# A decoder's self attentions: the fourth query tile finished in its own slot, the rotated keys taken one slot later

## The reference

```python
q = split_heads(x @ Wq)
k = split_heads(x @ Wk)
v = split_heads(x @ Wv)
q = _apply_rope(q, cos, sin)
k = _apply_rope(k, cos, sin)
scores = jnp.einsum('bhqd,bhkd->bhqk', q, k) * scale
scores = jnp.where(causal[None, None], NEG_INF, scores)
attn = jax.nn.softmax(scores, axis=-1)
ctx = jnp.einsum('bhqk,bhkd->bhqd', attn, v)
return ctx.reshape(b, s, H * HD) @ Wo
...
x = _layernorm(x + _L0_attn_ref(x, L0_attn_Wq, L0_attn_Wk, L0_attn_Wv, L0_attn_Wo), axis=-1)
```

## Time and profile before

| | |
|---|---|
| median of 3 runs | 2695.97 us (2695.12 to 2696.59) |
| profiled execution | 2701.27 us |
| its span | 2699.4 us |
| PE busy | 2454.4 us, 91% |
| DVE busy | 1853.7 us, 69% |
| ACT busy | 1586.2 us, 59% |
| POOL busy | 721.8 us, 27% |
| mean granted clock of PE | 0.964 |

### The profile page before, as it was taken

One profiled execution on the slowest core, in us unless ns is written; L12 is line 12 of the kernel. 1 busy time (PEld: TensorE's weight loads), 2 busy tenths in 40 slices (PEclk: granted clock), 3 DMA queues, 4 the chain that ended last, 5 costly groups with the idle time before them and its releaser, 6 DMA issues. The chain is left out here.

```text
span 2699.4 us, 58652 instructions
## 1 busy us (share of the span) xinstructions
PE 2454.4 (91%) x21584; PEld 1576.5 (58%) x21584; DVE 1853.7 (69%) x3371; ACT 1586.2 (59%) x2718; POOL 721.8 (27%) x671
## 2 busy tenths in 40 slices
PE   6888888989999999999778999999899999999974
PEld 4555555446666666666345666665466666665432
DVE  4676766657777777775556666666478888885597
ACT  4666666248778877785133555554167777774233
POOL 4565657611100111012233221214310000012201
PEclk8999998999999999999888999999999999999987
DMA  3333334516665566666340344335167777776400
GB/s 89 84 72 72 84 84 88 140 22 117 116 116 110 108 115 116 118 108 128 119 164 1 89 91 92 89 81 138 40 119 147 141 146 144 148 150 130 106 0 32
DMA packets 777604, 273.63 MB, mean 101 GB/s; under 512 B 746097, under 2 KB 748913, under 8 KB 775793
## 3 DMA queue, kind: packets, MB, share of 16 engines
q1 hardware_dynamic: 775696, 265.85, 46.8%
q0 software_dynamic: 1760, 5.77, 0.8%
HBM read 84.55 MB, written 6.44 MB: 34 GB/s over the span
## 5 line engine op out<-in xcount | busy, mean ns | idle before, releaser
L833 ACT ACTIVATE ph<-p,ri 128x1024 bf16<-128x1024 f32 (+4 forms) x512 | 437.4, 854 | 477.0 <-DVE ri L1139 398.1
L1149 DVE SCALAR_TENSOR_TENSOR pl<-p,ri,ph 128x1024 bf16<-128x1024 f32 (+4 forms) x512 | 511.9, 1000 | 141.4 <-issue 72.4
L1206 PE MATMUL ps<-wo_hi,v_hi 128*128 128x128 bf16 x2688 | 478.6, 220 | 59.7 <-DMA wo_lo<-pl 58.6
L1208 PE MATMUL ps<-wo_hi,v_lo 128*128 128x128 bf16 x2688 | 478.2, 220 | 0.0
L1207 PE MATMUL ps<-wo_lo,v_hi 128*128 128x128 bf16 x2688 | 478.1, 220 | 0.0
L844 ACT ACTIVATE p<-p,nb 128x1024 f32<-128x1024 f32 (+4 forms) x512 | 435.4, 850 | 46.3 <-DVE nb L1132 36.0
L1206 PEld LDWEIGHTS ps<-wo_hi,v_hi 128*128 128x128 bf16 x2688 | 263.5, 98 | 129.9 <-DMA wo_lo<-pl 80.7
L1206 PE MATMUL ps<-k_hi,q_hi 128*128 128x512 bf16 (+3 forms) x768 | 272.2, 354 | 36.9 <-DVE k_lo L1102 28.8
L1207 PEld LDWEIGHTS ps<-wo_lo,v_hi 128*128 128x128 bf16 x2688 | 263.7, 98 | 38.9
L1208 PE MATMUL ps<-k_hi,q_lo 128*128 128x512 bf16 (+3 forms) x768 | 271.9, 354 | 0.0
L1207 PE MATMUL ps<-k_lo,q_hi 128*128 128x512 bf16 (+3 forms) x768 | 271.9, 354 | 0.0
(11 more groups left out here) (191 smaller groups left out, 5831.8 us busy)
## 6 DMA issues: line engine op xcount, KB each, us to landing
raw_kv<-in_wkvself SPq DMA_DIRECT2D x32, 512.0 KB
raw_q<-in_wqself SPq DMA_DIRECT2D x32, 256.0 KB
wo_hi<-ph SPq DMA_TRANSPOSE x512
wo_lo<-pl SPq DMA_TRANSPOSE x512
raw_q<-in_woself SPq DMA_DIRECT2D x32, 256.0 KB
raw_q<-in_wqcross SPq DMA_DIRECT2D x32, 256.0 KB
raw_q<-in_wocross SPq DMA_DIRECT2D x32, 256.0 KB
raw_kv<-in_wkvcross SPq DMA_DIRECT2D x24, 256.0 KB
```

The costliest lines, as they stand in the source:

```text
L833: nc.scalar.activation(m["ph"][:, qt % 2, 0:w], m["p"][:, qt % 2, 0:w], ACT.Copy, scale=ri[:, qt % 2:qt % 2 + 1]).then_inc(p_norm, 1)
L1149: nc.vector.scalar_tensor_tensor(out=m["pl"][:, qt % 2, 0:w], in0=m["p"][:, qt % 2, 0:w], scalar=ri[:, qt % 2:qt % 2 + 1], in1=m["ph"][:, ...
L1206: nc.tensor.matmul(o, l(0), r(0), start=first, stop=False)
L1208: return nc.tensor.matmul(o, l(1), r(0), start=False, stop=last)
```

## The change

In the causal stages the fourth tile's `rounded` (ACT), `inverse` and `remainder` (DVE) move from slot 0 of the next unit to the end of slot 3 of their own, ahead of v and the head's output. In self0 the rotated key's `rotated` on ACT (k_hi) and on DVE (k_lo) moves from slot 2 to slot 3, behind `rounded` of tile 2 and behind `scores` of tile 3. The semaphore `tr_in[qt]` becomes two, `tr_hi[qt]` and `tr_lo[qt]`: `rounded` waits for the transposes of `ph` alone, `remainder` for those of `pl`, PE for both. `units` now runs 4 units ahead of the loop, 6 passes, and 4 units after it, in all stages with a loop.

```diff
-        tr_in = [sem(f"tr_in{i}") for i in range(QT)]
+        tr_hi, tr_lo = [sem(f"tr_hi{i}") for i in range(QT)], [sem(f"tr_lo{i}") for i in range(QT)]
...
-            unit(0, None)
-            with engine.Fori(0, 7) as it:
+            for n in range(4):
+                unit(n, None)
+            with engine.Fori(0, 6) as it:
                 for i in range(4):
-                    unit(1 + i, it)
-            for n in range(UNITS - 3, UNITS):
+                    unit(4 + i, it)
+            for n in range(UNITS - 4, UNITS):
                 unit(n, None)
...
(ACT, rounded)
-                        act.wait_ge(tr_in[bq], at(lambda n: 32 * (c["u"] + behind(n, qt, 2)[0] + 1), n, it))
+                        act.wait_ge(tr_hi[bq], at(lambda n: 16 * (c["u"] + behind(n, qt, 2)[0] + 1), n, it))
...
(ACT, unit)
-                        if n or qt:
+                        if qt or n and not L.causal:
                             rounded(*((n, it, qt - 1) if qt else (n - 1, it, QT - 1)))
+                        if L.rope and qt == QT - 1:
+                            rotated(n, it, 1, L.jobs(n, 1))
                         act.wait_ge(s_max, at(lambda n: CREDIT + c["s"] + QT * n + qt + 1, n, it))
...
+                        if L.causal and qt == QT - 1:
+                            rounded(n, it, qt)
                         job_parts(n, it, qt, L.jobs(n, qt))
                         if qt == QT - 1 and n:
                             heads_out(n - 1, it)
-                        if L.rope and qt > 0:
-                            rotated(n, it, qt - 1, L.jobs(n, qt - 1))
+                        if L.rope and qt == 1:
+                            rotated(n, it, 0, L.jobs(n, 0))
...
(DVE, unit)
-                        if n or qt:
+                        pending = qt or n and not L.causal
+                        if pending:
                             inverse(*prior)
                         scores(n, it, qt)
+                        if L.rope and qt == QT - 1:
+                            rotated(n, it, 1, L.jobs(n, 1))
                         job_parts(n, it, qt, L.jobs(n, qt), ("QN",))
-                        if n or qt:
+                        if pending:
                             remainder(*prior)
+                        if L.causal and qt == QT - 1:
+                            inverse(n, it, qt)
+                            remainder(n, it, qt)
                         job_parts(n, it, qt, L.jobs(n, qt), ("K", "KN", "Q", "V"))
                         if qt == QT - 1 and n:
                             heads_out(n - 1, it)
-                        if L.rope and qt > 0:
-                            rotated(n, it, qt - 1, L.jobs(n, qt - 1))
+                        if L.rope and qt == 1:
+                            rotated(n, it, 0, L.jobs(n, 0))
...
(PE, weigh)
-                    pe.wait_ge(tr_in[qt], at(lambda n: 32 * (c["u"] + n + 1), n, it))
+                    pe.wait_ge(tr_hi[qt], at(lambda n: 16 * (c["u"] + n + 1), n, it))
+                    pe.wait_ge(tr_lo[qt], at(lambda n: 16 * (c["u"] + n + 1), n, it))
```

More of the change, by code:

```diff
@@ L431, in transposed @@
                     sp.nop(nofuse=True)
-                    sp.dma_start_transpose(m["pT"][0][:, qt, 0:w // P, :], m["ph"][:, qt % 2, 0:w]).then_inc(tr_in[qt], 16)
+                    sp.dma_start_transpose(m["pT"][0][:, qt, 0:w // P, :], m["ph"][:, qt % 2, 0:w]).then_inc(tr_hi[qt], 16)
                     sp.wait_ge(p_lo, at(count, n, it))
                     sp.nop(nofuse=True)
-                    sp.dma_start_transpose(m["pT"][1][:, qt, 0:w // P, :], m["pl"][:, qt % 2, 0:w]).then_inc(tr_in[qt], 16)
+                    sp.dma_start_transpose(m["pT"][1][:, qt, 0:w // P, :], m["pl"][:, qt % 2, 0:w]).then_inc(tr_lo[qt], 16)
                 def unit(n, it):
@@ L863, in _ @@
                 units(act, unit, L)
-                rounded(UNITS - 1, None, QT - 1)
+                if not L.causal:
+                    rounded(UNITS - 1, None, QT - 1)
                 if L.name in EARLY:
@@ L1145, in remainder @@
                     if bn >= 0:
-                        dve.wait_ge(tr_in[bq], at(lambda n: 32 * (c["u"] + behind(n, qt, 2)[0] + 1), n, it))
+                        dve.wait_ge(tr_lo[bq], at(lambda n: 16 * (c["u"] + behind(n, qt, 2)[0] + 1), n, it))
                     dve.wait_ge(p_norm, at(lambda n: c["s"] + QT * n + qt + 1, n, it))
@@ L1180, in _ @@
                 units(dve, unit, L)
-                inverse(UNITS - 1, None, QT - 1)
-                remainder(UNITS - 1, None, QT - 1)
+                if not L.causal:
+                    inverse(UNITS - 1, None, QT - 1)
+                    remainder(UNITS - 1, None, QT - 1)
                 quantise_run(EARLY.get(L.name, ()))
```

## The result

| | before | after |
|---|---|---|
| median of 4 runs | 2696.28 us (2695.12 to 2699.3) | 2738.71 us (2731.98 to 2742.95) |
| profiled execution | 2701.27 us | 2731.98 us |
| its span | 2699.4 us | 2730.2 us |
| mean granted clock of PE | 0.964 | 0.960 |

The change makes the kernel slower: ratio 1.0153, interval 1.0131 to 1.0176. The prediction said 2728 us, within 2706 to 2742; the median is 10.7 us above the number and inside the range. The profiled execution of the change is the fastest of its four, and that of before took longer than any of its four, so the profiled executions differ by 30.7 us and the medians by 42.4.

The account below looks back on a forecast made before the run. Self0 was taken as bound by a loop over DVE, ACT and POOL, self1 by PE. Self0 +36.8 and self1 -5 gave +31.8 on 2701.3, so 2733 profiled and, 5.3 lower, a median of 2728 us, range 2706 to 2742.

Parts of the forecast that it names:

- A unit with splits: Self0 units with POOL weight splits: k_lo falls behind wkv_lo and is stalled; 13.66 becomes 15.77 us, +2.1 us each.
- A unit without splits: Self0 units without POOL weight splits: the period goes from 13.16 to 13.67 us, +0.5 us each.
- a chain of waits served on the spot: Self0, fourth tile's exponential, inverse, `ph`, remainder: waiting there costs more than the 0.4 us freed at the unit's front.
- Self0: First self attention: 27.3 for 13 split units, 1 for unit 1, 8.5 for 17 others; +36.8 us, bounds +16 and +45.
- rival 4: Self0: PE falls to its lower clock after idling for the late k_lo; +7 to +14 us, 2735 to 2742; chance 0.1.
- Self1: Second self attention, paced by PE: a quarter of its transpose wait is gained, -5 us, bounds 0 and -22.
- the gain can only come from the 21.8 us: Self1: only PE's 21.8 us wait for the transposed remainders can shrink.
- inside this number: Self1: split transpose waits serve ACT a little earlier, counted within the -5 us.
- Rival 1: Self0: k_lo slips in ahead of wkv_lo; self0 +16 to +29, total 2707 to 2720 us; chance 0.2.
- Rival 2: Transposes set self0's pace and the time falls, by up to 37 us; 2659 to 2690 us; chance 0.09.
- Rival 3: A draw: self0 +16 or a little less, self1 -15; total 2691 to 2701 us; chance 0.05.
- Other stages 0: Cross attentions' extra PE wait is on an already full semaphore, and peeled units move no work: 0.

Follow-up runs that it names:

- e5: The change with POOL's subtraction wkv_lo left out in all units of self0: 2722.28 us, ratio to before 1.0081.
- e3: Kernel before with two semaphores, peeled units and, in self0 only, the rotated keys in slot 3: 2702.51 us, ratio to before 1.0027.
- e2: Kernel before with two semaphores, peeled units and, in self0 only, the fourth tile finished in its own slot: 2726.11 us, ratio to before 1.0112.
- e10: As e2, but the fourth tile's steps stand behind v and the head's output: 2708.38 us, ratio to before 1.0038.
- the control: Also written e1: the change with both moves undone, two semaphores and four peeled units kept: 2690.09 us, ratio to before 0.9979.
- e9: Kernel before with the two semaphores alone, its loop unchanged: 2694.65 us, ratio to before 0.9983.
- e4: Kernel before with two semaphores, peeled units and, in self1 only, the fourth tile finished in its own slot: 2693.53 us, ratio to before 0.999.
- e8: As e3, with POOL's wq splits moved to slot 2 and wkv's to slot 3: 2673.53 us, ratio to before 0.9902.

## Why the prediction was right, and where not

The total, 2728 us, lay 10.7 under the median; the way it came about was forecast for self0 and failed for self1. In the traced executions the two stages together grew by 38.0 us where +31.8 was forecast, and all the rest was 7.2 us shorter, 4.3 of it in the stage behind self0. That the traced execution of the change, 2732 us, met the 2733 named for it is therefore partly luck.

- **A unit with splits: 15.77 forecast, 15.64 measured in unit 13.** By the clock that starts with the unit's scores: k_lo at 9.59 (9.62 forecast), its end at 11.97 (12.04), the remainder of tile 2 at 11.90 (11.97), inverse 12.78 (12.88), remainder of tile 3 at 13.77 (13.88), v_lo 14.44 (14.55), oT_lo 15.04 (15.17). The mechanism stood in unit 1 of the trace of before, and e5, where k_lo falls to 0.75 us without wkv_lo, shows it is wkv_lo. By the rule of the Trainium skill (SBUF — State Buffer, Who interferes with whom) nothing of k_lo runs before wkv_lo ends; it ended 0.54 us after it, where it takes 0.69 alone, so the row was the better price, by 0.15 us. That the one that starts later is held up is borne out in each split unit: k_lo took 2.32 to 2.38 us in all 14.
- **A unit without splits: 13.67 forecast, 13.61 to 13.76 measured.** But the forecast netted two moves of opposite sign: the keys alone gain 0.6 us there (e3), the fourth tile alone costs 0.6 to 0.7 (e2). The reason given, a chain of waits served on the spot, is the smaller part of it: e10 puts v_lo and oT_lo between the links and still pays 0.55 us, since the remainder has left a wait of DVE that hid it.
- **Self0: +36.8 forecast, +39.2 measured.** Period by period, the 13 split units behind unit 1 gave +25.9 us (27.3 forecast), unit 1 +1.5 (1), the other 17 +14.1 (8.5), and what follows the last unit's first exponential -2.3 (nothing forecast). The 14.1 is 5.6 over the forecast, most of it in units that PE's lower clock stretched (rival 4 below). The upper bound given for self0, +45, is +44 by its own terms (36.8 + 14 x 0.5). The parts, in total time over the control: the fourth tile in self0 +36 us, the keys +12, the fourth tile in self1 +3, in sum 52, where the change as a whole has +49. Within a unit the parts don't add (split units: +1.8 and +0.9, together +1.9; free units: +0.65 and -0.6, together +0.45), so the near agreement of the sums is partly luck.
- **Self1: -5 forecast, -1.2 measured, and its reason was wrong.** The step that failed is "the gain can only come from the 21.8 us" and the -5 us taken from SP's pauses. PE's wait for the transposes did fall, to 16.6 us in the change, but the control without the move has 16.4. The gain came with the two semaphores, which cut ACT's 61.7 us of waiting for the transposes of `pl` to 28.9 (e9; -4 to -5 us in self1 there and in e1), and which the prediction had put "inside this number". The earlier fourth tile costs 3.4 us of the total instead (e4). With it DVE waits 38.4 us for the buffer (7.7 in the control), which the prediction had not looked at, though the text on the kernel names the wait.
- **Rival 1** (k_lo slips in ahead of wkv_lo) is out: k_lo took 2.3 to 2.4 us in the split units. **Rival 2** (the transposes set the pace) is out too: PE's wait for them fell from 29.5 to 8.4 us, and self0 is longer. **Rival 3**, a draw, as well.
- **Rival 4**, PE's lower clock, came true beside the forecast, at a smaller size. Between units 2 and 30 of self0, PE had 20 waits of over 1.8 us (11 before), and behind 10 of them the 512-column matmuls took 0.63 us (behind 1 before); 0.94 was the mean clock (0.97), and PE's busy time grew by 6.8 us, between the two signs given (unchanged for the forecast, over 10 us for the rival). The stretched units add up to 6 us over the periods that the others keep. The forecast had this at +7 to +14. The other runs of the change lie 6.5 to 11 us above the profiled one, and their mean granted clock was lower, 0.955 to 0.959 against 0.960, lowest in the longest. More such units in them would fit that, but no trace shows them, and it is left open.
- "Other stages 0" holds: the cross attentions took 665.9 and 497.1 us, 665.5 and 497.9 before.

## What to carry to other kernels

Work that is off the path is hidden only where it stands: before moving a step "to where it belongs", look at which wait covers it now, and what the engine next door runs at the new place. When two engines stall each other, moving the cheap side (here POOL's splits) did more than any order of the expensive one that was tried alone: with it the keys' move gave a ratio of 0.9902, without it 1.0027. And undo the parts one by one: this change held one part worth keeping (two semaphores), one that pays only once its neighbour is moved (the keys), and one that paid in no version tried (the fourth tile).

## What the runs showed of the hardware

- An instruction of DVE with two SBUF inputs that starts behind one of POOL's splits isn't fully blocked by it: k_lo (0.69 us alone) ended 0.54 us after wkv_lo in the change. It works the other way as well: wkv_lo took 2.12 us when it started ahead of DVE's k_lo, and 2.44 in unit 13 of before, where it started at 225.75 while k_lo was running. That k_lo had itself been held up, to 1.03 us, by wkv_hi (224.46 to 225.68), in every split unit of before but unit 1:

```profile
225.18 1.03 DVE L1102 TENSOR_TENSOR k_lo<-rot,k_hi 128x512 bf16<-128x512 f32 x1 [0.41 <-ACT k_hi L813]
```

- The same idle time of PE doesn't always lower its clock. In e3, PE idled 3.18 us for k_lo in units 7, 11, 15, 19 and 23, and the matmuls behind it took 0.63 us in units 11 and 19 and 0.38 in the other three. In e2, with nine waits of 2.0 us, five were followed by slow matmuls, though no unit got longer by it. In the control, whose waits were 1.8 to 1.9 us but for the last unit's, and in e8, which had only one of over 1.8 us, no 512-column matmul between units 2 and 30 was slow behind one.
